# Moving one batch of shared-expert products behind the routed blocks, and the last second norm to the vector engine

## The reference, cut to what matters

```python
mod = (_silu(L0_c) @ L0_wmod)...            # six vectors a batch; ga and gb are kept away from 0
h = _layernorm(x) * (1 + ca) + sa
x = x + ga * attention(h)                    # 16 heads, causal
h = _layernorm(x) * (1 + cb) + sb            # the "second norm"
x = x + gb * ffn(h)

def ffn(x):
    aff = sigmoid(x @ wa)                    # router: 16 experts
    topk_p, topk_i = top_k(aff, 2); topk_p = topk_p / sum(topk_p)
    routed = sum over the 2 chosen experts of p * expert(x)
    shared = sum over 2 shared experts of expert(x)
    return x + shared + routed
# expert(x) = (gelu(x @ g + gb) * (x @ w1 + b1)) @ w2 + b2, with 512 -> 256 -> 512
```

## Time and profile before

| | |
|---|---|
| median of 3 runs | 1478.45 us (1478.17 to 1478.78) |
| profiled execution | 1476.72 us, of which the span of the trace is 1475.1 us |
| PE busy | 1366.7 us, 93% |
| DVE / ACT / POOL busy | 840.2 / 671.3 / 376.8 us |
| mean granted clock of PE | 0.97 |

### The profile page before, as it was taken

One profiled execution on the slowest core, in us unless ns is written; L12 is line 12 of the kernel. 1 busy time (PEld: TensorE's weight loads), 2 busy tenths in 40 slices (PEclk: granted clock), 3 DMA queues, 4 the chain that ended last, 5 costly groups with the idle time before them and its releaser, 6 DMA issues. The chain is left out here.

```text
span 1475.1 us, 23417 instructions
## 1 busy us (share of the span) xinstructions
PE 1366.7 (93%) x7100; PEld 1159.0 (79%) x7100; DVE 840.2 (57%) x1715; ACT 671.3 (46%) x1551; POOL 376.8 (26%) x304
## 2 busy tenths in 40 slices
PE   7889893899999999999999999996998899999993
PEld 6666672788888888888888888885887787887872
DVE  5676653555666666566676666664554443443448
ACT  3233322756666665666667656662321232222222
POOL 0324342000002145012370032702826000000034
PEclk9999996999999999999999999997999999999997
DMA  9998797698888668786699766865459688888257
GB/s 301 327 384 316 249 367 288 210 369 309 294 307 309 218 216 285 264 305 218 204 362 368 277 222 200 278 220 193 169 194 334 236 317 313 311 315 328 101 202 254
DMA packets 174794, 403.12 MB, mean 273 GB/s; under 512 B 23992, under 2 KB 81276, under 8 KB 162432
## 3 DMA queue, kind: packets, MB, share of 16 engines
q1 hardware_dynamic: 157440, 305.89, 59.3%
q0 software_dynamic: 17280, 96.28, 17.4%
HBM read 250.56 MB, written 151.55 MB: 273 GB/s over the span
## 5 line engine op out<-in xcount | busy, mean ns | idle before, releaser
L1116 ACT ACTIVATE a_pr<-a_pr,a_stat 128x128 f32<-128x128 f32 (+3 forms) x256 | 142.0, 556 | 115.3 <-DVE a_stat L1187 114.7
L1284 PEld LDWEIGHTS a_psY<-a_pT,a_cv 128*128 128x128 f32 x768 | 123.8, 188 | 15.5 <-issue 2.1
L1284 PE MATMUL a_psY<-a_pT,a_cv 128*128 128x256 f32 (+2 forms) x768 | 134.1, 323 | 1.9 <-DVE a_pT L1206 1.9
L1187 DVE CUSTOM_DVE_ANT_0 a_pr<-a_psS,a_mask 128x128 f32<-128x128 f32 (+3 forms) x256 | 114.7, 487 | 30.0 <-PE a_psS L1272 29.6
L1122 ACT ACTIVATE a_pr<-a_pr,a_stat 128x128 f32<-128x128 f32 (+3 forms) x256 | 122.1, 548 | 0.0
L102 PE MATMUL a_psX<-a_hT,a_wqk 128*128 128x512 f32 (+1 forms) x256 | 101.0, 394 | 13.4 <-POOLq L1066 13.4
L1132 ACT ACTIVATE a_oT<-a_psY 128x512 fp32r<-128x512 f32 x64 | 38.2, 596 | 153.1 <-PE a_psY L1284 153.1
L1217 DVE TENSOR_TENSOR n_acc<-a_psZ,n_acc 128x512 f32<-128x512 f32 x125 | 86.4, 691 | 35.8 <-PE a_psZ L104 33.9
L1201 DVE TENSOR_TENSOR a_oT<-a_psY,a_oT 128x512 fp32r<-128x512 f32 x64 | 44.2, 691 | 105.6 <-ACT a_oT L1132 105.5
L103 PE MATMUL a_psX<-a_hT,a_wqk 128*128 128x512 f32 (+1 forms) x256 | 101.0, 395 | 0.0
L104 PE MATMUL a_psX<-a_hT,a_wqk 128*128 128x512 f32 (+1 forms) x256 | 100.9, 394 | 0.0
(11 more groups left out here) (305 smaller groups left out, 3464.6 us busy)
## 6 DMA issues: line engine op xcount, KB each, us to landing
w1s_d<-a_ws SPq DMA_DIRECT2D x72, 512.0 KB, 3.6
a_wqk<-wqk_d SPq DMA_DIRECT2D x64, 512.0 KB, 4.8
a_mh<-mhl_d SPq DMA_DIRECT2D x32, 1024.0 KB, 7.2
s_ring<-w1s_d POOLq DMA_DIRECT2D x13, 2048.0 KB, 8.9
w2s_d<-a_ws SPq DMA_DIRECT2D x72, 256.0 KB, 4.3
qpe_d<-p_qs SPq DMA_DIRECT2D x16, 1024.0 KB, 5.5
a_qpe<-qpe_d SPq DMA_DIRECT2D x64, 256.0 KB, 3.5
a_rw<-in_L_ffn_rw SPq DMA_DIRECT2D x128, 128.0 KB, 3.6
```

The source lines that it names most:

```text
L1116: nc.scalar.activation(pr[i], pr[i], ACT.Exp, bias=nmax[:, i:i + 1], scale=-1.0, accum_out=rsum[:, i:i + 1]).then_inc(ex, 1)
L1187: nc.vector.tensor_tensor_reduce(out=pr[i], in0=score[i][:, 0:w], in1=mask[:, S - w:S], scale=-1.0, scalar=3e38, op0=ALU.add, op1=ALU.min, ...
L1284: m = nc.tensor.matmul(psY[:, q0:S], cv[:, j, cs], pT[:, ps, o:o + w], start=n == 0, stop=n == 11)
```

## The change

What it does:

1. Batch 2's shared products move from ahead of the routed blocks to behind those of batch 3. The order of batches in `hT`, in the counters and in the output is now 0, 1, 3, 2 (`nth`, `order_t`). As `hT` of batch 2 would sit in the weight ring, it is written to DRAM (`h2T_d`, 2 MB) and read back into slot 1 after the last block. Its update becomes `complete`, added straight to the finished output tile.
2. Batch 3's second norm is done by DVE in `stage_ffn` (`added`, `normed`), but for the power, which POOL computes (`rstd`). The base stays on POOL, as three wide operations (`base`), begun when the norm is done (`h3_ok`).
3. Transposes and routers of all batches are placed among the first shared products of batch 0; `order` follows the last `second` of batch 0.
4. SP's loads are put in a new order to suit: ring slots 0 and 2 after batch 0, slot 1 and the second ring's slots 1 and 2 after batch 1.
5. The combination of tiles is interleaved with two batches of shared products: `tiles_m` is now a list for each of the two batches.

```diff
+    def added(self, dve, freed):
+        tt = self.K.nc.vector.tensor_tensor
+        for i in range(TB):
+            m = tt(self.t[:, i], self.acc[:, i], self.rows[:, 0], ALU.mult).then_inc(self.vch, 1)
+        dve.wait_ge(self.vch, TB)
+        dve.sem_inc(freed, 1)
+        for i in range(TB):
+            m = tt(self.x[:, i], self.t[:, i], self.x[:, i], ALU.add)
+        m.then_inc(self.x1_ok, 1)
+    def normed(self, dve, i, ready):
+        v = self.K.nc.vector
+        if i == 0:
+            dve.wait_ge(self.rs_ok, 1)
+        h, n = self.h[:, i], TB + 3 * i
+        v.tensor_scalar(h, self.x[:, i], self.mv[:, i, 0:1], self.rs[:, i:i + 1], ALU.subtract, ALU.mult).then_inc(self.vch, 1)
+        dve.wait_ge(self.vch, n + 1)
+        v.tensor_tensor(h, h, self.rows[:, 2], ALU.mult).then_inc(self.vch, 1)
+        dve.wait_ge(self.vch, n + 2)
+        v.tensor_tensor(h, h, self.rows[:, 1], ALU.add).then_inc(self.vch, 1)
+        if i == TB - 1:
+            dve.wait_ge(self.vch, n + 3)
+            dve.sem_inc(ready, 1)
...
+        nth = {0: 0, 1: 1, LAST: 2, 2: 3}
+        order_t = [b * TB + t for b in nth for t in range(TB)]
+        turn = lambda c, b: nth[b] * DC + c
...
-        tiles_m = [[], [0, 1], [2, 3], [4, 5]]
-        tiles_t = [[6, 7], [8, 9], [10, 11], [12, 13]]
-        tiles_e = [14, 15]
+        tiles_m = {LAST: [[], [0], [1, 2], [3, 4]], 2: [[10, 11], [12, 13], [14], [15]]}
+        tiles_t = [[5], [6], [7], [8, 9]]
...
             def _(pool):
                 nc.gpsimd.memset(ones[:, :], 1.0).then_inc(zero, 1)
-                N.steps(pool, LAST, 0, N.x[:, :, :], acc_free, h3_ok)
+                N.rstd(pool, 0)
+                pool.wait_ge(h3_ok, 1)
+                N.base(pool)
...
             def _(dve):
+                N.added(dve, acc_free)
+                for i in range(TB):
+                    N.stats_of(dve, 0, i)
                 for c in range(DC):
                     h_low(0, c)
+                N.stats(dve, 0, False)
...
+                for i in range(2):
+                    N.normed(dve, i, h3_ok)
+                for m, b in enumerate((1, LAST, 2)):
+                    h_low(b, 0)
+                    h_low(b, 1)
+                    if m == 0:
+                        N.normed(dve, 2, h3_ok)
+                        N.normed(dve, 3, h3_ok)
                     times(0, m)
                     y_low(0, m)
+                    h_low(b, 2)
+                    h_low(b, 3)
...
-                for m in range(NU):
-                    times(2, m)
-                    y_low(2, m)
                 for b in range(B):
                     dve.wait_ge(xs_out[b], 16 * TB * TOP)
...
+                def complete(t):
+                    i, n = 3 * TB + t, nth[2] * TB + t
+                    dve.wait_ge(sh_o, n + 1)
+                    tt_(ys[:, t % 2], po[:, t % 2], gb4[:, 2], ALU.mult).then_inc(so_ok, 1)
+                    dve.wait_ge(so_ok, n + 1)
+                    dve.wait_ge(part, t + 1)
+                    tt_(at[:, i % NA], at[:, i % NA], ys[:, t % 2], ALU.add).then_inc(o_ok, 1)
...
             def _(pe):
-                for m in range(NU):
-                    first_(2, m, 0, gate)
-                    first_(2, m, 1, up)
...
+                pe.wait_ge(h2T_in, 16)
+                for m in range(NU):
+                    first_(2, m, 0, gate, late)
+                    first_(2, m, 1, up, late)
+                for t in range(TB):
+                    second(2, t)
```

More of the change, by code:

```diff
@@ L852, in steps @@
         tiles(h, h, row(1), ALU.add, ch.sem)
[L853 to L857, removed]
[L858 to L859 removed]
+        pool.dma_start(K.h2_d[b * S:(b + 1) * S].rearrange("(t p) n -> p t n", p=P), h[:, :, :]).then_inc(self.h2_out, 16)
@@ new lines, in steps, with rstd, base @@
+        tiles(t, h, lambda i: self.b2[:, :], ALU.add, ch.sem)
+        tiles(t, t, row(3), ALU.mult, ch.sem)
+        tiles(x, x, tile_of(t), ALU.add, ch.sem)
+    def rstd(self, pool, n):
+        pool.wait_ge(self.var_ok, n + 1)
+        self.K.nc.gpsimd.tensor_tensor(self.rs[:, :], self.ve[:, :], self.half[:, :], ALU.pow).then_inc(self.rs_ok, 1)
+        pool.wait_ge(self.rs_ok, n + 1)
+    def base(self, pool):
+        ch, tt = self.chain, self.K.nc.gpsimd.tensor_tensor
+        wide = lambda a: a.broadcast_to([P, TB, D])
+        ch.after(tt(self.t[:, :, :], self.h[:, :, :], wide(self.b2[:, :].unsqueeze(1)), ALU.add))
+        ch.after(tt(self.t[:, :, :], self.t[:, :, :], wide(self.rows[:, 3:4]), ALU.mult))
+        ch.after(tt(self.x[:, :, :], self.x[:, :, :], self.t[:, :, :], ALU.add))
@@ L1944, in _ @@
                     combine(tiles_t[t])
-                combine(tiles_e)
+                for m in range(NU):
+                    times(2, m)
+                    y_low(2, m)
+                    combine(tiles_m[2][m])
+                for t in range(TB):
+                    complete(t)
             @block.tensor
@@ L2040, in _ @@
                 x_trans(LAST, 1)
+                router(0)
+                first_(0, 1, 1, up)
+                by_token(0)
+                x_trans(LAST, 2)
+                x_trans(LAST, 3)
+                first_(0, 2, 0, gate)
+                router(1)
+                pe.wait_ge(hx_in[0], 32)
+                x_trans(2, 0)
+                x_trans(2, 1)
+                first_(0, 2, 1, up)
+                by_token(1)
+                router(LAST)
+                x_trans(2, 2)
+                x_trans(2, 3)
+                first_(0, 3, 0, gate)
+                by_token(LAST)
                 router(2)
                 first_(0, 3, 1, up)
-                x_trans(LAST, 2)
-                x_trans(LAST, 3)
                 by_token(2)
-                second(0, 0)
-                router(LAST)
-                second(0, 1)
-                by_token(LAST)
-                second(0, 2)
-                second(0, 3)
+                for t in range(TB):
+                    second(0, t)
+                order()
                 for m in range(NU):
```

307 lines of the change are left out of this document (143 added, 164 removed).

## The result

The changed kernel takes 1496.14 us (median of 4 runs, 1495.56 to 1497.75) where the kernel before takes 1478.37 (1478.17 to 1478.78): a ratio of 1.0122, 95% interval 1.0104 to 1.0139. That is 17.8 us slower; 1495 was forecast. The profiled execution took 1497.75 us, its span 1496.1.

A forecast was written before the change was run, and what follows sets the result against it. Bounds: PE in the routed blocks, POOL's 32 spread issues in the head (covered by batch 2's products), DVE at the end. Tail +23.2 less head 6.5 gave +16.7 us, so 1495 us; range 1482 to 1506.

The forecast's parts named there:

- The stall: Before PE's turn 8 transposes: DVE's norm and POOL's base delay `y_low`, 6.7 us lost, 8.8 with the low clock.
- The bound of 3.3 us: Same place, if POOL does not hold up `y_low`: only 3.3 us lost; as a rival, chance 0.13.
- The small waits: Around batch 0's seconds: less work covers `times`, copy and `y_low`, and `best` delays an update: 0.9 and 0.5 us.
- Places: End of DVE's chain behind batch 0's last second and `order`: at 1098.6, 3.9 us later than before.
- last spread: The last of POOL's 32 indirect DMA issues behind the places: at 1140.1, the first at 1099.0.
- Landing to first block product: Ahead of the blocks: spread landed at 1144.4, first block's load at 1147.4, first block product at 1151.2.
- Blocks: Routed blocks: work untouched and carried over, 257 us, but 2.1 us lost to the low clock at their start.
- Head, net: Up to the blocks: they begin 8.6 us earlier, less 2.1 us of low clock, giving 6.5 us.
- The end: Behind the blocks, with batch 3's and batch 2's products: 81.4 us, 23.2 more than 58.2.
- The three signs of being wrong: PE idle under 8 us before the blocks, batch 3's transposes before 1044, or a tail shorter than 75 us.
- the faster one: Rival on the spread: full queues, not POOL, hold its 32 issues, so it speeds up: 1465 to 1474, chance 0.07.
- the slow first load: Rival ahead of the blocks: crowded queues make the load 8.8 us for 2.8, spread slower: 1504, chance 0.10.

The follow-up runs named there:

- e4: Changed kernel with batch 2's shared products put back ahead of the routed blocks, the rest of the change kept: 1490.97 us, ratio to before 1.0078.
- e3: Kernel before the change with 16 spread issues instead of 32, the second expert's copies left out: 1478.42 us, ratio to before 0.9987.
- e1: Changed kernel with batch 3's four transposes one product half later and `logits(0)` moved to match: 1494.67 us, ratio to before 1.0101.
- e2: Changed kernel with 16 spread issues instead of 32, the second expert's copies left out: 1485.84 us, ratio to before 1.0045.

## Why the prediction was right

The sum was right by its terms, not only in total, with one stroke of luck.

- *The stall*: 6.7 us forecast, 6.37 measured, with the stretched `y_low` beside GpSimd's wide operation, and the low clock behind it. The bound of 3.3 us for GpSimd not holding up `y_low` was near too: 3.84 us when it doesn't. That the whole head would be 8.8 and 1.4 us longer by the norm and the routers is what e4 isolates: 9.4 us for 10.2.
- *The small waits*: 0.9 and 0.5 forecast; 1.24 less the 0.37 of before, and 0.26. How much of the first is the change's is not sure: in e3, whose head is before's, this wait was 1.19.
- *Places* 1098.6 and *last spread* 1140.1 forecast; 1099.07 (end of the last cast) and 1140.42 measured. Less the 2.4 us by which the stage began later, that is 1096.7 and 1138.0, so some 2 us before the forecast. This is the luck: after's first products ran at full clock, where before's ran at the low one, and the two cancel in the absolute times.
- *Landing to first block product*: 4.3 + 2.8 + 3.8 forecast, 6.9 + 2.7 + 4.5 measured, so 1154.51 for 1151.2, or 1152.1 less the 2.4. The missed 2.6 us is the landing: the 4.3 was read from before's last spread, under other traffic. Of the 3.8, 2.3 were read from a row and the rest was called handovers.
- *Blocks*: 257 forecast, and 2.1 us for the low clock. 259.7 measured, which holds the low clock (0.50 over the first 4.9 us); waits for weights were 7.4 us where before had 6.6.
- *Head, net*: 6.5 us given back forecast. Measured: 7.8 less the 2.4 us of the blocks, so 5.4, of which some 2 us are the luck of the clock.
- *The end*: +23.2 forecast, +23.9 measured. The terms written down add up to 81.2 us and not 81.4, which changes nothing. The waits are 4.3 and 3.3 instead of 3.0 and 3.0. The row below fits the first: VectorE waits for the sum's read for the first combination, which SP asked for right behind the 2 MB read of batch 2's transposes and which landed 15.6 us later.

```profile
1431.62 0.69 DVE L1974 TENSOR_TENSOR s_at<-s_at,n_acc 128x512 f32<-128x512 f32 x1 [2.81 <-DMA n_acc<-sum_d]
```

The three signs of being wrong stayed away: PE stood idle for 18.6 us before the blocks (under 8 was the sign), batch 3's transposes start at 1048.24 (before 1044), the end takes 81.9 us (under 75). A side remark of the prediction is wrong, and nothing rests on it: that stall and later places eat 12.7 us counts the stall twice, since the 3.9 us by which the places are later hold it already.

Of the rivals, the faster one (issues held by queues) falls by the even pace of 1.32 us through the lighter head, and the slow first load by its 2.7 us. What the prediction implied and the runs refute is that the stall's 8.8 us could be had back by themselves: moving the transposes returned 1.5 us by medians, 3 by ratios, since VectorE is late a second time, again beside a wide base operation of GpSimd.

What stays open is the other chips. There no cost of after against before can be told (1.0014, 0.9988 to 1.0041). A partial reason is in the traces. From the first chip to these, e4's order (head 140.2, end 57.7) grew to 160.1 and 74.2 us in the run with the later transposes, 36.4 together; after's (123.0 and 81.9) to 137.1 and 91.3, 23.5 together, and its idle gap shrank (12.24 us left of 18.56), so some of the lost time may have fallen into it. No trace of before exists there, so that this holds for before itself is argued, not shown.

## What to carry to other kernels

Work that seems to be only in front of a stage may be the cover of a chain on another engine: before it is moved, lay the chain (here places, 32 issues, landing, first load: 51 us) against the work that stays. A removed wait is worth the distance to the next one: here 6.4 us of waiting held 2.5 that could be removed by moving the transposes; 2.2 reached the blocks, and 1.5 to 3 us, within the noise, the end. And an engine that is given work in front of its own handovers passes it on: here 3.9 us of norm in front of VectorE's low parts (1038.33 to 1042.24) stood behind 3.8 us of TensorE's wait, and what `y_low` met beside GpSimd's wide operation made it 6.4.

## What the runs showed of the hardware that I had not expected

- On two chips VectorE, ScalarE and TensorE lost time while the spread and the gathers ran, and the profile names no engine of this core that would have released them (`remote`): PE waits of 10.9 to 29.9 us ahead of batch 1's seconds where the first chip has 2.3, and on VectorE in the same stretch, in after:

```profile
1127.27 0.75 DVE L1798 SCALAR_TENSOR_TENSOR s_y<-s_pg,s_bT,s_y 128x512 f32<-128x512 f32 x1 [12.10 <-remote]
1144.22 0.69 DVE L1816 TENSOR_TENSOR s_y<-s_po,s_gb 128x512 f32<-128x512 f32 x1 [14.81 <-remote]
```

  GpSimd, which issues the spread, kept its pace (40.7 us from first to last issue in this run). Before took 38 us more on one of these chips than in the first measurement (1516.5 for 1478.4), and a change of 1.2% on one chip could not be told from none on another. What holds the engines there no run shows, and that before's 38 us are such gaps isn't shown either, as it has no trace there.
- The low clock does not follow the length of the wait alone: PE came out of 1.24 us at batch 0's seconds at full clock in after's order (0.50 us for the first matmul) and in e1 at the low one (0.77), and 3.31 us at 1479.41 was followed by a full clock first (0.96 over 1.2 us) and a low one then (0.54 over the next 3.6 us).
- The landing of the last indirect spread of 128 rows took 4.3 us in before, with no weights asked for in the 30 us ahead of it, and 6.1 to 7.8 us in e4, after, e3, e1 and e2, with 2 MB or more of weights asked for within 25 us. That the weights are the reason no run isolates.
